# Narrow attentions with separate PSUM rings: four banks in pairs for the row scores, three single banks for the column scores of one head

## What is computed

```python
# third layer, causal
scores = einsum('bhqd,bhkd->bhqk', q_rot, k_rot) / sqrt(8)
scores = scores - abs(i - j) / xi * e_gate
scores = where(causal, scores, -inf)
out = einsum('bhqk,bhkd->bhqd', softmax(scores), v)
# fourth layer, without a mask
scores = einsum('bhqd,bhkd->bhqk', q, k) / sqrt(8)
o = einsum('bhqk,bhkd->bhqd', softmax(scores), v)
```

## Time and profile before

| | us |
|---|---|
| median of 3 runs | 4987.53 |
| lowest, highest | 4985.31, 4990.92 |
| the profiled execution | 4995.73 |
| its span, first to last instruction | 4993.8 |

### The profile page before, as it was taken

One profiled execution on the slowest core, in us unless ns is written; L12 is line 12 of the kernel. 1 busy time (PEld: TensorE's weight loads), 2 busy tenths in 40 slices (PEclk: granted clock), 3 DMA queues, 4 the chain that ended last, 5 costly groups with the idle time before them and its releaser, 6 DMA issues.

```text
span 4993.8 us, 110824 instructions
## 1 busy us (share of the span) xinstructions
PE 4390.7 (88%) x41476; PEld 2162.2 (43%) x41514; DVE 3925.8 (79%) x4589; ACT 3299.4 (66%) x7123; POOL 2915.9 (58%) x2205
## 2 busy tenths in 40 slices
PE   6998888859999999999999999968888888888847
PEld 2333333335555555555555555543333322222226
DVE  5899888958888888788878986757666778888721
ACT  5565566427777878787778777744555566767734
POOL 4888888946888888688867866833222203110024
PEclk9999999979999999999999999988999999999968
DMA  4555555513334334334434343341211110110015
GB/s 149 190 187 182 182 187 186 194 41 92 111 103 120 109 103 124 84 108 111 124 88 106 102 115 85 91 106 43 46 34 43 28 27 27 25 29 14 2 39 173
DMA packets 258821, 488.46 MB, mean 98 GB/s; under 512 B 58731, under 2 KB 108398, under 8 KB 257636
## 3 DMA queue, kind: packets, MB, share of 16 engines
q1 hardware_dynamic: 255288, 475.05, 33.0%
q0 software_dynamic: 3008, 6.32, 0.3%
HBM read 435.33 MB, written 35.30 MB: 94 GB/s over the span
## 4 chain that ended last, share of the span: by engine, by line
PE 62%; DVE 12%; issue 11%; ACT 10%; POOL 2%; DMA 1%; SPq 1%; POOLq 0%; DVEq 0%; ACTq 0%
PE ps L2352 9%; PE ps L1456 7%; PE ps L1416 7%; PE ps L1446 7%; PE ps L1402 7%; PE ps L548 4%; PE ps L2323 4%; PE ps L2305 3%; ACT n_P L2387 3%; PE ps L495 2%; DVE shared L1746 2%; PE ps L1395 2%; ACT s_P L1576 2%; DVE ps L713 1%; DVE m_HH L728 1%
## 5 line engine op out<-in xcount | busy, mean ns | idle before, releaser
L2466 DVE TENSOR_REDUCE n_MX<-ps 128x2 f32<-128x1024 f32 (+6 forms) x1034 | 982.8, 980 | 239.1 <-PE ps L2305 135.3
L2387 ACT ACTIVATE n_P<-ps 128x1024 f32<-128x1024 f32 (+4 forms) x1022 | 826.0, 838 | 449.4 <-PE ps L2323 233.8
L1576 ACT ACTIVATE s_P<-s_P,s_MB 128x256 f32<-128x256 f32 x2048 | 1012.4, 511 | 0.2
L1561 ACT ACTIVATE s_P<-ps 128x1024 f32<-128x1024 f32 x512 | 526.4, 1029 | 410.6 <-PE ps L1416 395.6
L1729 DVE TENSOR_REDUCE s_MX<-s_P 128x4 f32<-128x1024 f32 x512 | 600.2, 1211 | 204.9 <-ACT s_P L1561 203.8
L771 POOL TENSOR_TENSOR m_PR<-m_HH,m_CS 128x1024 f32<-128x1024 f32 x256 | 606.7, 2386 | 152.1 <-issue 126.6
L1746 DVE STREAM_TRANSPOSE shared<-s_P 128x1024 f32<-128x1024 f32 x512 | 627.3, 1229 | 34.8 <-ACT s_P L1576 34.4
L1957 POOL TENSOR_TENSOR s_OG<-s_OG,s_OT 128x1024 f32<-128x1024 f32 x256 | 609.4, 2381 | 14.5 <-DMA s_OG<-s_gt 14.5
L1416 PE MATMUL ps<-s_QF 64*32 64x256 f32 x16384 | 509.8, 384 | 55.0 <-DVE XTB L1720 20.4
L1974 POOL TENSOR_TENSOR XTB<-XTB 128x512 f32<-128x512 f32 x256 | 329.0, 1285 | 390.6 <-DVE XTB L1720 390.3
L1456 PE MATMUL ps<-s_OG,s_WO 128*128 128x512 f32 x1024 | 514.1, 625 | 26.7 <-POOL s_OG L1957 22.5
(11 more groups left out here) (358 smaller groups left out, 6656.8 us busy)
## 6 DMA issues: line engine op xcount, KB each, us to landing
m_CS<-m_rows_c SPq DMA_DIRECT2D x256, 512.0 KB
s_OG<-s_gt SPq DMA_DIRECT2D x512, 256.0 KB, 4.3
m_BS<-m_rows_c SPq DMA_DIRECT2D x80, 512.0 KB
s_WV<-in_s_v SPq DMA_DIRECT2D x32, 512.0 KB, 4.0
s_TA<-XTB SPq DMA_DIRECT2D x256, 64.0 KB, 3.3
s_WO<-in_s_o SPq DMA_DIRECT2D x32, 512.0 KB, 5.4
s_OR<-s_sums SPq DMA_DIRECT2D x128, 128.0 KB, 4.4
g_WB<-in_g_wx SPq DMA_DIRECT2D x23, 578.0 KB
```

The costliest lines, as they stand in the source:

```text
L1576: ins = s.activation(P, P, ACT.Exp, bias=self.MB[:, g // 2 % 2, at % 16:at % 16 + 1], accum_out=self.SU[:, g // 4 % 2, at:at + 1])
L2387: ins = s.activation(P[:, at:at + x.shape[1], lo:512], x[:, :, lo:512], ACT.Exp, scale=scale)
L2466: ins = v.tensor_reduce(self.MX[:, q, at:at + x.shape[1], hp, t], x[:, :, 0:width], AX.X, ALU.max)
```

## The change

`Pairs` now gets four banks (0 to 3), that is two places of two banks, for row steps and all other steps but col. A new class `Line` hands out banks 4, 5 and 6 one by one to the halves (one head each) of the col steps. Each half has its own wait, its own matmul, its own semaphore increment and its own exponential of at most 512 columns. So PE's mask matmuls of a diagonal col step now stand behind their head's score matmul, not alternating between the heads. Half number i waits until half i-3 has been read. The values step, SyncE's loads and `finish` get matching waits. In the phase before, one semaphore is saved by counting three memsets on one.

```diff
--- before.py
+++ after.py
@@ -121,6 +121,34 @@
 
     def take(self, step):
         return self.read[self.reader[step]], 1
+
+
+class Line:
+
+
+    def __init__(self, nc, ctx, name, slots, uses):
+        self.slots = slots
+        self.full, self.read = (ctx.enter_context(nc.semaphore(f"{name}_{x}")) for x in ("full", "read"))
+        self.at = {s: i for i, s in enumerate(uses)}
+
+    def ap(self, step):
+        return self.slots[self.at[step] % len(self.slots)]
+
+    def empty(self, e, step):
+        if self.at[step] >= len(self.slots):
+            e.wait_ge(self.read, self.at[step] - len(self.slots) + 1)
+
+    def filled(self, e, step):
+        e.wait_ge(self.full, self.at[step] + 1)
+
+    def taken(self, e, step):
+        e.wait_ge(self.read, self.at[step] + 1)
+
+    def fill(self):
+        return self.full, 1
+
+    def take(self):
+        return self.read, 1
 
...
@@ -1925,10 +1953,10 @@
     def gpsimd(self, g):
         n = self.n
         self.own_p = own = Own(g, self.c.own_g)
-        g.memset(self.MX[:, :, :], 0.0).then_inc(self.mx_zero, 1)
-        g.memset(self.MR[:, :, :], 0.0).then_inc(self.mx_zero, 1)
         g.memset(self.TA[:, 1, :], 0.0).then_inc(self.zeroed, 1)
-        g.wait_ge(self.zeroed, 1)
+        g.memset(self.MX[:, :, :], 0.0).then_inc(self.zeroed, 1)
+        g.memset(self.MR[:, :, :], 0.0).then_inc(self.zeroed, 1)
+        g.wait_ge(self.zeroed, 3)
         g.wait_ge(self.consts_in, 16 * 5)
@@ -2022,10 +2050,12 @@
         c.root_count = c.norm_count
         c.norm_count += len(self.norm)
         self.OB = c.ps[:, 3584:4096]
-        engine = {"rows": "s", "qk2": "v", "v": "v", "row": "v", "max_t": "s", "col": "s", "finish": "v",
+        engine = {"rows": "s", "qk2": "v", "v": "v", "row": "v", "max_t": "s", "finish": "v",
                   "out_t": "s", "out": "v"}
         who = lambda s: ("v" if s[1] < NB else "s") if s[0] == "qk" else engine[s[0]]
-        self.r = Pairs(nc, ctx, "n_psum", c.ps, 7, [(s, s[0] in ("row", "col"), who(s)) for s in self.steps if s[0] in engine or s[0] == "qk"])
+        self.r = Pairs(nc, ctx, "n_psum", c.ps, 4, [(s, s[0] == "row", who(s)) for s in self.steps if s[0] in engine or s[0] == "qk"])
+        self.cols_at = Line(nc, ctx, "n_cols", [c.ps[:, u * 512:u * 512 + 512] for u in (4, 5, 6)],
+                            [(*s, hh) for s in self.steps if s[0] == "col" for hh in range(2)])
         self.last_col = {s[1]: s for s in self.steps if s[0] == "col"}
         self.last_row = {(s[1], s[2] // 2): s for s in self.steps if s[0] == "row"}
         self.loaded = {}
@@ -2214,7 +2244,7 @@
                              self.PT[:, 3 * side:3 * side + 3, :]).then_inc(self.parts_out, 16)
             elif kind == "load":
                 if n > 2:
-                    r.taken(sp, self.last_col[n - 3])
+                    self.cols_at.taken(sp, (*self.last_col[n - 3], 1))
                 unit_rows(sp, self.c, W, n, self.QS[n % 3], self.KS[n % 3], self.base(n), self.qk_in[n % 3])
             elif kind == "consts":
                 for dst, src in ((self.wf[:, :, :], W["f_w"]), (self.lnp[:, :, :], W["f_lnp"].partition_broadcast(128)),
@@ -2310,23 +2340,22 @@
                 ins = pe.matmul(self.r.half(step, hh)[:, width - 128:width], self.EM[hs, a, :], self.EM[hs, 2 + a, :], start=False, stop=a == 1)
         ins.then_inc(*self.r.fill(step))
 
-    def col(self, pe, step, ps):
+    def col(self, pe, step):
 
         n, hp, t, q = step[1:]
         Q, K, k = self.QS[n % 3], self.KS[n % 3], self.base(n) + 3
         pe.wait_ge(self.m_in, 96 * (2 * n + hp // 2 + 1))
-        self.r.empty(pe, step)
         lo = max(t * 128 if n < 8 else 0, 512 * q)
         diag = n < 8 and t // 4 == q
         for hh in range(2):
-            hs = slice(64 * hh, 64 * hh + k)
-            ins = pe.matmul(self.r.half(step, hh)[:, lo - 512 * q:512], K[hs, hp, t * 128:(t + 1) * 128],
+            place, hs, ms = self.cols_at.ap((*step, hh)), slice(64 * hh, 64 * hh + k), slice(64 * hh, 64 * hh + 64)
+            self.cols_at.empty(pe, (*step, hh))
+            ins = pe.matmul(place[:, lo - 512 * q:512], K[hs, hp, t * 128:(t + 1) * 128],
                             Q[hs, hp, lo:512 * q + 512], start=True, stop=not diag)
-        for a in range(2 if diag else 0):
-            for hh in range(2):
-                hs, at = slice(64 * hh, 64 * hh + 64), lo - 512 * q
-                ins = pe.matmul(self.r.half(step, hh)[:, at:at + 128], self.EM[hs, a, :], self.EM[hs, 4 + a, :], start=False, stop=a == 1)
-        ins.then_inc(*self.r.fill(step))
+            for a in range(2 if diag else 0):
+                at = lo - 512 * q
+                ins = pe.matmul(place[:, at:at + 128], self.EM[ms, a, :], self.EM[ms, 4 + a, :], start=False, stop=a == 1)
+            ins.then_inc(*self.cols_at.fill())
 
     def values(self, pe, step):
         n, hp, t = step[1:]
@@ -2334,7 +2363,7 @@
         causal = n < 8
         for q in range(2):
             if not causal or t < 4 * q + 4:
-                self.r.taken(pe, ("col", n, hp, t, q))
+                self.cols_at.taken(pe, ("col", n, hp, t, q, 1))
         if t == 0:
             pe.wait_ge(self.zero_g, 6)
             if s > 0:
@@ -2378,15 +2407,13 @@
             elif kind == "col":
                 hp, t, q = step[2:]
                 lo = max(t * 128 - 512 * q, 0) if n < 8 else 0
-                r.filled(s, step)
                 k = 32 * n + 8 * hp + t
                 if k >= 3:
                     s.wait_ge(self.values_done, k - 2)
-                P, at = self.P[(32 * n + 8 * hp + t) % 3][q], 0
-                for x in ps:
-                    ins = s.activation(P[:, at:at + x.shape[1], lo:512], x[:, :, lo:512], ACT.Exp, scale=scale)
-                    at += x.shape[1]
-                ins.then_inc(*r.take(step))
+                for hh in range(2):
+                    self.cols_at.filled(s, (*step, hh))
+                    s.activation(self.P[k % 3][q][:, hh, lo:512], self.cols_at.ap((*step, hh))[:, lo:512], ACT.Exp,
+                                 scale=scale).then_inc(*self.cols_at.take())
             elif kind == "copy":
                 k = n_(*step)
                 s.wait_ge(self.values_done, 8 * k)
@@ -2477,6 +2504,8 @@
             elif kind == "finish":
                 g, hp, s = n % 2, step[2], n // 2
                 r.filled(v, step)
+                if 4 * n + hp > 0:
+                    r.taken(v, ("finish", *divmod(4 * n + hp - 1, 4)))
                 p = ps[:, 0:512].rearrange("p (t c h r) -> p c t h r", t=4, c=2, h=2)
                 rs = self.RS[:, :].rearrange("p (c t h) -> p c t h", c=2, t=4)
                 for q in range(2):```

How many instructions the list gives to each engine in the whole program: ACT's exponentials were 1022 and are 1792 (two for each of 896 col steps); the row maxima were 1034 and are 896 (one for each row step).

On PE, in the units without a mask, one col, row and values step before (L2323 col, L2305 row, L2352 values; "shared", n_QS and n_KS are query and key tiles):

```order
L2323 MATMUL ps<-shared 128x512 [waits n_psum_read_s,n_psum_read_v,n_m_in]
L2323 MATMUL ps<-shared 128x512
L2305 MATMUL ps<-n_KS,n_QS 128x512 [waits n_psum_read_s,n_psum_read_v,n_qk_in1]
L2305 MATMUL ps<-n_KS,n_QS 128x512
L2352 MATMUL ps<-n_P,n_VA 32x512 [waits n_psum_read_s]
L2352 MATMUL ps<-n_P,n_VA 32x512 x3
```

More of the change, by code:

```diff
@@ L899, in __init__ @@
         for name in ("consts_in", "zeroed", "ln_chain", "ln_out", "top_v", "own_top", "b2_done", "spill_out", "top_done", "gates_out", "gv_out", "raw_done", "swap_in", "turn_done",
-                     "rope_done", "wq_in", "wv_in", "gvj_in", "v_done", "mx_zero", "mx_done", "flipped", "most_done", "bias_full", "bias_read", "exp_done",
+                     "rope_done", "wq_in", "wv_in", "gvj_in", "v_done", "mx_done", "flipped", "most_done", "bias_full", "bias_read", "exp_done",
                      "pt_done", "values_done", "o_done", "su_out", "su_in", "recip_done", "sums_out", "or_in", "ot_done", "og_done", "wo_in", "onto_done", "outt_done", "wf_in", "xn_in", "aff_done",
@@ L1421, in tensor @@
                 g = self.tile(*step[1:]) // 2
-                pe.wait_ge(self.mx_zero, 2)
+                pe.wait_ge(self.zeroed, 3)
                 pe.wait_ge(self.mx_done, 2 * (g + 1))
@@ L1722, in vector @@
                 g = self.tile(*step[1:])
-                v.wait_ge(self.mx_zero, 2)
+                v.wait_ge(self.zeroed, 3)
                 if g > 3:
@@ L2271, in tensor @@
             elif kind == "col":
-                self.col(pe, step, ps)
+                self.col(pe, step)
             elif kind == "values":
```

## The result

The changed kernel takes 4,964.4 us (median of 4 runs, 4,956.0 to 4,968.9), the kernel before on the same chip 4,988.5 (4,985.3 to 4,990.9): a ratio of 0.9946, interval [0.9934, 0.9958]. In a second set, on another chip, it took 4,961.4, ratio 0.9942 [0.9928, 0.9955]. So it is 24 us faster by the medians and 27 by the ratio, with an interval from 21 to 33; 16.6 us slower was forecast, and the time is that of rival C.

The account below looks back on a forecast made before the run. Without a mask ACT's reads hold PE, DVE close behind; in causal units' second halves PE's streaming bounds. Halves -10.6, masks +27, rest 0: +16.6 us on 4,987.5 gives 5,004, range 4,960 to 5,030 (forecast's own 4,993 to 5,017, 43%).

Parts of the forecast that it names:

- rival C: Irregular stretches: col steps no longer see DVE's extra work; 42 us gained there, sum -25, 4,962; chance 29%.
- Part 2: Diagonal col steps, causal stage: masks per head add w + 128 columns each; +0.85 us a head pair, +27 us.
- Part 1: Col steps in halves, without a mask: plain period 5.37 to 5.26 us, 96 x 0.11 = 10.6 us gained.
- I: Start-to-start distance of ACT's exponentials of 512-column halves, taken as 0.50 us; plain period 4.26 + 2I.
- C1: Start of the col behind the second values in a plain period without a mask, taken as time zero.
- Part 3: The rest: row maxima, places for other steps, memsets' semaphores, extra waits; 0 each, extra waits at most 9 us.
- B: About nothing: the diagonal's extra columns hide behind waits or the heads overlap better; -7 us, 4,980; chance 15%.
- D: ACT's halves start 0.75 us apart, masks included +64, 5,051; by the skill page 0.72, +59, 5,046; chance 10%.
- E: Causal stage: weight loads of the masks exposed in full, 99 us more, 5,103; chance 3%.

Follow-up runs that it names:

- The first experiment: Kernel before, one edit: in diagonal col steps PE gets one head's score matmul and two masks, then the other head's; 4,993.9 against 4,991.9, 1.0003.

## Why the prediction was wrong

**Part 2, the masks, is the step that failed.** It said that head 1's score matmul "stands in order behind head 0's last mask", and took w + 128 columns per diagonal step, +27 us. The first experiment gives 1.5 us (-3 to +6), the trace 0.35 us from col to row where 0.53 was named as the sign, and the causal stage, which had to be longer for the forecast to hold, is 7 us shorter. A matmul did not wait for one of the other row group that stands ahead of it, so the two heads' chains ran side by side in both orders of the program. The lower bound of the term, 0, was right. Its size alone turned the sign.

**Part 1 had the right mechanism and a size that was too small.** The waits stand where the prediction put them: in front of a second half, none of a row for ACT, with I = 0.49 to 0.50 on ACT. But from the end of an exponential to the matmul that it releases I took 0.15, read in front of a whole row step. In front of a second half it is 0.05: the first exponential of the six ends at 4445.93 + 0.60 = 4446.53, and the half starts at 4446.58. So the third col's second half starts 2.11 after C1 (4447.16 + 0.79 - 0.39 = 4447.56) and not 2.18. The row's first head is 0.10 behind it, its second head still 0.22, and from there to the next C1 all is as forecast: 5.18 and not 5.26. 96 x 0.19 = 18 us in place of 10.6. The finish period, put at no gain, gains 6.08 - 5.91 = 0.17, and 32 x 0.17 = 5. Check: a plain head pair has three periods of the one and one of the other, 3 x 0.19 + 0.17 = 0.74, and 22.19 - 21.45 is the 0.74 measured. The plain head pair behind it gains 1.1, which the sum does not have. The experiment with two exponentials shows the price that was paid beside it: the instructions cost 25 us where halves bring nothing, against the bound of 9 by which I = 0.60 could have hurt.

**Part 3.** Extra waits and semaphores show nothing. The places for rows and projections cost nothing that shows, but I did not see the end: the last two head pairs lose 4 to 5 us. With only col steps left three banks hold less than seven did, and one ring in halves, with seven, keeps these pairs at 18.9 and 18.8.

**The rivals.** The masks at 0 and the periods as measured give -18 - 5 = -23. The stages changed by -7 and -29, -36 in all (-39 in the second set), and the span by -27, with the start of the phase 10 us later by chance in the profiled execution. So 13 to 16 us lie outside the plain pattern, and 18 to 20 before the loss in the last two head pairs; the sum had put this part at nothing. C said 42 there. The experiment with DVE's wait back shows C's mechanism at 20 us, none of it in plain head pairs and up to 12 of it by way of the clock (last section). B named the masks' fate rightly and missed the rest. D and E are excluded: halves start 0.49 apart, neither 0.75 nor the 0.72 of D's second price, and the first experiment bounds the loads at 6 us. That C's time was right is luck: less came from its own mechanism, and the plain pattern and the masks made up the difference.

**What the separation was for.** Neither wait put back alone tells that two rings are needed: one ring in halves has the DVE wait and is faster. What the runs show as necessary is the half as the unit of waiting; without it two rings take 5,017.8 and not 4,961.4, and one ring 5,016.9 and not 4,947.5. It lets ACT be fed while the other bank is not yet free. How the 14 us between the two divide among the shorter period (5.06 against 5.18), the tail and the side work was not taken apart.

## What to carry to other kernels

Before pricing a reordering of matmuls, ask which row group each uses: here chains in different row groups cost the longer of the two, not their sum in program order. Read the time from a release to the start that it allows in front of the same kind of instruction as the one to be priced (0.05 and 0.15 here). When a small ring of PSUM banks stalls PE, split the unit of waiting before splitting the ring, and follow the wait of each half. An edit that helps beside one arrangement of banks can undo the gain beside another (4,951 and 4,947 apart, 4,994 together), so such edits are to be run together before they are believed.

## What the runs showed of the hardware

The start of a later matmul ahead of an earlier one of another row group (3905.57 and 3905.61; by 0.22 us in the kernel with the second head behind the row, at 4503.54) was not expected. The Trainium skill (TensorE: Matmul & The Clock Gate, Part 3, on what overlaps) describes matmuls as starting and ending in program order; these traces differ, by 0.04 and 0.22 us, and the measured price of the masks follows the traces.

PE's granted clock falls to its lower level (0.5, 1.2 GHz) more often in kernels that stall more. In the kernel with DVE's wait back, the clock in two neighbouring windows:

```profile
4499.00:4504.00 5.00, 3.26 (x26) 1.13 (x18) 4.08 (x8) 3.71 (x7) 0.00 (x0) 0.95 0.00 0
4504.00:4509.00 5.00, 4.71 (x24) 0.79 (x24) 3.20 (x4) 2.29 (x5) 0.00 (x0) 0.50 0.00 0
```

PE was busy for 3.26 of the 5 us ahead of the fall, and a values step then took 1.93 us instead of 1.06. Summed over the stage without a mask, the lower level was granted for 44 us before, 34 and 27 in the two profiles of the changed kernel, 51 with DVE's wait back and 75 with ACT's. A microsecond at half the clock costs at most half of one, so up to (44 - 27) / 2 = 8 us of the change's gain, and up to 12 of the 20 us of DVE's wait, may come by way of the clock.

Head pairs repeat so exactly that the same one can be compared with and without the lower level. In the kernel with the masks per head the first plain head pair takes 23.00 us with none of it and, at the next place of its kind, 24.59 with 3.4 us of it; with DVE's wait back another takes 24.30 with none and 26.38 with 6.8. So a microsecond at the lower level costs 0.3 to 0.5, which puts 5 to 8 us of the gain and 7 to 11 of DVE's wait on the clock. With DVE's wait back, the 48 of 63 head pairs that are at full clock in it and in the changed kernel's second profile lose 5 us together and the other 15 lose 14. If the waits are what brings the lower level on, as the windows above suggest, this is part of what a wait costs and not a cause apart; no run here holds the clock fixed to show it.
